# A fused two-layer transformer kernel: token rows spread by DMA, doubled weight buffers, and more of the attention's maxima in the first stage

## The reference

```python
xn = layernorm(x)                                  # no gain, no bias
# first layer, attention branch: 16 heads of width 8, rotary positions
Q, K, V = rope(xn @ Wq.T), rope(xn @ Wk.T), xn @ Wv.T
s = softmax(causal(Q @ K.T / sqrt(8))) @ V @ Wo.T
# first layer, gate branch: feed-forward with weights that depend on the batch
lt   = xn[:, 1:17, :]; even, odd = lt[:, ::2], lt[:, 1::2]          # 8 rows each
m1   = (even[:, :4, :, None] * odd[:, :4, None, :]).reshape(B, 512, 128)
m2   = (even[:, 4:, :, None] * odd[:, 4:, None, :]).reshape(B, 128, 512)
h    = gelu(xn @ W1.T + scale * xn @ m1.T + b1)
g    = silu(h @ W2.T + scale * h @ m2.T + b2)
x    = x + s * g
# second layer: retention with decay, and a mixture of 8 experts (top 2, capacity); x = x + s2 * silu(experts)
```

## Time and profile before

| | |
|---|---|
| Time, 3 runs | 978.13 us median (975.89 to 981.47) |
| Profiled execution, its own time | 978.77 us |
| Its span in the profile | 977.0 us |
| PE busy | 856.4 us (88%) |
| DVE busy | 801.8 us (82%) |
| ACT busy | 725.9 us (74%) |
| POOL busy | 289.4 us (30%) |
| First block | 0 to about 122 us |
| First score product of the second block | 141.93 us |

### The profile page before, as it was taken

How to read it: one execution, slowest core, us unless ns; L and a number is a source line. 1 busy time by engine, 2 the same in 40 slices (tenths; PEclk the granted TensorE clock), 3 DMA queues, 4 the chain that set the end, 5 groups by cost and what they waited for, 6 DMA issues and landing times. The chain is left out here.

```text
span 977.0 us, 25280 instructions
## 1 busy us (share of the span) xinstructions
PE 856.4 (88%) x9413; PEld 459.8 (47%) x9414; DVE 801.8 (82%) x1697; ACT 725.9 (74%) x1493; POOL 289.4 (30%) x329
## 2 busy tenths in 40 slices
PE   3999989899999999999998899888999999889960
PEld 3666533333333333333334777533444444368850
DVE  6665899899999999999963664599999999837895
ACT  2655338788888888888886555688999999958841
POOL 3866311111111000000013676501444442005560
PEclk9999959999999999999999899889999999989985
DMA  5469691744444363333006778596654442546727
GB/s 172 184 261 342 261 219 49 212 103 104 107 104 106 70 137 69 71 67 73 13 14 179 247 236 246 143 224 131 111 118 89 100 82 49 139 147 219 206 104 260
DMA packets 119385, 140.92 MB, mean 144 GB/s; under 512 B 20109, under 2 KB 82138, under 8 KB 118624
## 3 DMA queue, kind: packets, MB, share of 16 engines
q1 hardware_dynamic: 113888, 127.45, 48.3%
q0 software_dynamic: 5376, 11.85, 4.2%
HBM read 77.63 MB, written 63.25 MB: 144 GB/s over the span
## 5 line engine op out<-in xcount | busy, mean ns | idle before, releaser
L980 ACT ACTIVATE probsB<-psB 128x512 f32<-128x512 f32 (+2 forms) x640 | 309.5, 569 | 69.9 <-PE psB L1037 45.1
L174 DVE TENSOR_REDUCE mxB<-psB 128x1 f32<-128x512 f32 x428 | 246.1, 645 | 11.5 <-PE psB L151 8.1
L1030 PE MATMUL psB<-q_groups,k_groups 64*128 64x512 bf16 (+3 forms) x768 | 203.6, 331 | 17.6 <-DVE mxB L174 8.3
L151 PE MATMUL psB<-k_groups,q_groups 64*128 64x512 bf16 (+2 forms) x740 | 206.4, 339 | 2.0 <-PEq L408 1.8
L1058 PE MATMUL psB<-probsB,vB 128*32 128x512 f32 (+3 forms) x1536 | 164.9, 501 | 1.3 <-ACT outB L967 0.6
L1870 ACT ACTIVATE psD<-psD 128x896 f32<-128x896 f32 (+2 forms) x192 | 153.5, 799 | 8.5 <-PE psD L1924 8.3
L1030 PEld LDWEIGHTS psB<-q_groups,k_groups 64*128 64x128 bf16 x768 | 66.8, 94 | 160.9 <-ACT probsB L980 140.2
L1799 DVE TENSOR_REDUCE sumsD<-psD 128x1 f32<-128x128 f32 (+3 forms) x256 | 113.4, 484 | 7.2 <-PE psD L1947 5.0
L1924 PE MATMUL psD<-k_groups,q_groups 64*128 64x512 bf16 (+3 forms) x384 | 103.2, 341 | 13.5 <-ACT psD L1870 5.4
L174 DVE TENSOR_REDUCE mx2B<-psB 128x2 f32<-128x256 f32 (+3 forms) x188 | 102.7, 597 | 11.7 <-PE psB L158 9.6
L158 PE MATMUL psB<-hideB,chooseB 64*128 64x128 bf16 x984 | 108.5, 207 | 0.0
(11 more groups left out here) (239 smaller groups left out, 1551.2 us busy)
## 6 DMA issues: line engine op xcount, KB each, us to landing
v<-vaugA SPq DMA_DIRECT2D x4, 2048.0 KB, 8.8
vB<-v SPq DMA_DIRECT2D x16, 512.0 KB
q_groups<-q SPq DMA_DIRECT2D x32, 200.0 KB
k_groups<-k SPq DMA_DIRECT2D x32, 200.0 KB
back<-emptyB POOLq DMA_DIRECT2D x16, 256.0 KB, 3.8
q<-hiA SPq DMA_DIRECT2D x12, 256.0 KB, 6.6
k<-hiA SPq DMA_DIRECT2D x12, 256.0 KB, 5.9
q_groups<-q SPq DMA_DIRECT2D x32, 96.0 KB
```

The source lines that it names most:

```text
L151: ins = nc.tensor.matmul(bank[:, to:to + w], self.q[r, s, a, t * P:t * P + P], self.k[r, s, a, HALF * c:HALF * c + w], start=True, stop=(c ...
L174: return nc.vector.tensor_reduce(dst, src, AX.X, ALU.max)
L980: nc.scalar.activation(probs[:, n % DEEP, 0:w], st[ring_of(n)][:, 0:w], ACT.Exp, scale=DH ** -0.5).then_inc(exp_done, 1)
L1030: ins = nc.tensor.matmul(bank[:, to:to + w], k[half[r], s, hq // 2, jt * P:jt * P + P], q[half[r], s, hq // 2, i0:i0 + w], start=True, sto ...
```

## The change

- `outer`, its constant and its load are gone. ACT issues two transfers for each batch: one stores the 8 rows from `xn` to DRAM (after the second tile of `normalise`), one reads them back to all partitions of a new tile `first` (`spread_first`). `weights` takes `first` in place of the PSUM banks; both of its tensor operands are then in SBUF.
- `w1e` and `w2e` have two buffers. On DVE `weights(b)` comes right after `rope(b, 0)`, ahead of `statistics(b+1)`; for the first batch it comes ahead of `rope(0, 0)`. PE does `project(0, 1)` inside the first feed-forward.
- `project` waits for one half of `xnT` a product. ACT runs one gelu at the start, and the gelus of the first half batch come ahead of the cast of `hi`.
- 32 units of maxima are in the first block. Units 0 to 7 are in feed_forward(2, 1), in banks 0 and 1 alone; DVE reads them after `weights(3)`. Each pair of them waits until the pair before it has been read. The other 24 stand where 24 stood.
- `vaug` and its DRAM copy have 16 columns a head in place of 32; the weight load of the products with the values still takes 32 columns, and so the next head's 16 as well. A load brings eight pieces of 256 bytes a partition. POOL clears the 16 columns behind the last head.
- DVE's clearing of the tile moves with `EARLY`, to ahead of the 17th unit counted from 32, which is behind the cast L888. In the fourth block the first load of values is issued by ACT.

```diff
+VC = 2 * DH
...
-EARLY = 24
+EARLY, EARLIEST = 32, 8
...
-        w1e, w2e = m.sb("w1eA", [P, FF]), m.sb("w2eA", [P, FC, P])
+        w1e, w2e = m.sb("w1eA", [P, 2, FF]), m.sb("w2eA", [P, 2, FC, P])
...
-        early_banks = [ps[:, i, :] for i in (0, 1, 4, 5)]
+        early_bank = [ps[:, n % 2, :] for n in range(EARLIEST)] + [ps[:, (0, 1, 4, 5)[n % 4], :] for n in range(EARLIEST, EARLY)]
...
                 def weights(b):
                     dve.wait_ge(xnT_ready, 2 * b + 1)
                     V.tensor_scalar(odd[:, :], xnT[:, b % 2, 2:18:2], scale[:, 0:1], None, ALU.mult).then_inc(odd_ready, 1)
-                    dve.wait_ge(outer_done, b + 1)
-                    if b:
-                        dve.wait_ge(u_done, 2 * b)
+                    dve.wait_ge(first_moved, 32 * (b + 1))
+                    if b >= 2:
+                        dve.wait_ge(u_done, 2 * b - 2)
                     dve.wait_ge(odd_ready, b + 1)
                     for j in range(4):
                         c = slice(j * P, j * P + P)
-                        V.scalar_tensor_tensor(w1e[:, c], ps[:, 0, c], odd[:, j:j + 1], w1[:, c], ALU.mult, ALU.add)
+                        V.scalar_tensor_tensor(w1e[:, b % 2, c], first[:, c], odd[:, j:j + 1], w1[:, c], ALU.mult, ALU.add)
                     for j in range(4):
                         o = slice(j * 32, j * 32 + 32)
-                        ins = V.scalar_tensor_tensor(w2e[:, :, o], ps[:, 1, j * P:j * P + P].rearrange("p (r q) -> p q r", q=FC),
+                        ins = V.scalar_tensor_tensor(w2e[:, b % 2, :, o], first[:, HALF + j * P:HALF + j * P + P].rearrange("p (r q) -> p q r", q=FC),
                                                      odd[:, 4 + j:5 + j], w2[:, :, o], ALU.mult, ALU.add)
                     ins.then_inc(w_ready, 1)
...
+                def read_early(first, last):
+                    for n in range(first, last):
+                        dve.wait_ge(groups.max_done, n + 1)
+                        groups.read_maximum(nc, 0, MAX_UNITS[n], early_bank[n]).then_inc(groups.max_read, 1)
...
                 for b in range(B):
                     if b:
                         add_bias(b - 1, 0)
+                    if b == 0:
+                        weights(b)
                     rope(b, 0)
-                    if b == 0:
+                    if b:
                         weights(b)
                     if b + 1 < B:
                         statistics(b + 1)
+                    if b == B - 1:
+                        read_early(0, EARLIEST)
                     if b:
                         add_bias(b - 1, 1)
-                        weights(b)
                     rope(b, 1)
...
-                read_early(0, EARLY // 2)
+                read_early(EARLIEST, EARLIEST + 12)
...
+                        if t == 1:
+                            act.wait_ge(xn_ready, NT * b + 1)
+                            act.dma_start(A["first"][b].rearrange("o (j c) -> (o j) c", c=D), xn[1:17:2, 0, :]).then_inc(first_moved, 16)
+
+                def spread_first(b):
+                    act.wait_ge(first_moved, 32 * b + 16)
+                    if b:
+                        act.wait_ge(w_ready, b)
+                    act.dma_start(first[:, :], A["first"][b].broadcast_to((P, 8 * D))).then_inc(first_moved, 16)
...
+                act.wait_ge(ready, 1)
+                nc.scalar.activation(warm[:, :], eps[:, :], ACT.Gelu)
                 normalise(0)
+                spread_first(0)
                 columns(0)
                 act.wait_ge(ready, 5)
                 act.wait_ge(loaded, 16 * (len(consts) + 2))
                 for b in range(B):
                     keep_v(b)
+                    gelu(b, 0)
                     if b == 0:
                         first_part(0, 0)
-                    gelu(b, 0)
                     if b + 1 < B:
                         normalise(b + 1)
                         columns(b + 1)
                     first_part(b, 1)
                     second_part(b, 0)
+                    if b + 1 < B:
+                        spread_first(b + 1)
                     second_part(b, 1)
...
-                def outer(b):
-                    for j in range(8):
-                        ins = nc.tensor.matmul(ps[:, j // 4, (j % 4) * P:(j % 4) * P + P], pick[:, j, :], xn[:, 0, :],
-                                               start=True, stop=True)
-                    ins.then_inc(outer_done, 1)
-
                 def project(b, half):
                     for j in range(2):
+                        pe.wait_ge(xnT_ready, 2 * b + (1 + j if half == 0 else 2))
                         ins = nc.tensor.matmul(ps[:, 4 + j, :], w_proj[:, j, :], xnT[:, b % 2, halves[half]], start=True, stop=True)
                     ins.then_inc(projected, 1)
...
-                    if n == 2:
+                    if n == EARLIEST + 2:
                         pe.wait_ge(terms_ready, 2 * B)
-                    if n >= 4:
-                        pe.wait_ge(groups.max_read, n - 2)
-                    side_by_side(*(groups.fill_maximum(nc, 0, MAX_UNITS[i], early_banks[i % 4], groups.max_done) for i in (n, n + 1)))
+                    if n:
+                        pe.wait_ge(groups.max_read, n if n <= EARLIEST else n - 2)
+                    side_by_side(*(groups.fill_maximum(nc, 0, MAX_UNITS[i], early_bank[i], groups.max_done) for i in (n, n + 1)))
 
                 def feed_forward(b, half):
                     first = 2 * FC * b + FC * half
                     for c in range(FC):
+                        if b == B - 2 and half == 1 and c % 2:
+                            two_maxima(c - 1)
                         if b == B - 1 and half == 1:
-                            two_maxima(8 + 2 * c)
+                            two_maxima(EARLIEST + 8 + 2 * c)
                         if first + c >= 2:
                             pe.wait_ge(gelu_done, first + c - 1)
-                        nc.tensor.matmul(ps[:, 2 + c % 2, :], w1e[:, c * P:c * P + P], xnT[:, b % 2, halves[half]],
+                        nc.tensor.matmul(ps[:, 2 + c % 2, :], w1e[:, b % 2, c * P:c * P + P], xnT[:, b % 2, halves[half]],
                                          start=True, stop=True).then_inc(h_done, 1)
+                    if b == half == 0:
+                        pe.wait_ge(terms_ready, 1)
+                        project(0, 1)
                     pe.wait_ge(v_kept, 2 * b + half + 1)
                     for t in range(4):
+                        if b == B - 2 and half == 1 and t % 2:
+                            two_maxima(4 + t - 1)
                         if b == B - 1:
-                            two_maxima(16 * half + 2 * t)
+                            two_maxima(EARLIEST + 16 * half + 2 * t)
                         for c in range(FC):
                             if t == 0:
                                 pe.wait_ge(gelu_done, first + c + 1)
                             ins = nc.tensor.matmul(ps[:, 6 + half, t * P:t * P + P], hT[:, c, t * P:t * P + P],
-                                                   w2e[:, c, :], start=(c == 0), stop=(c == FC - 1))
+                                                   w2e[:, b % 2, c, :], start=(c == 0), stop=(c == FC - 1))
                     ins.then_inc(u_done, 1)
                 pe.wait_ge(loaded, 16 * (len(consts) + 2))
                 turn_rows(0)
-                outer(0)
-                pe.wait_ge(xnT_ready, 2)
                 project(0, 0)
                 values(0)
-                pe.wait_ge(terms_ready, 1)
-                project(0, 1)
                 for b in range(B):
                     pe.wait_ge(w_ready, b + 1)
                     feed_forward(b, 0)
                     if b + 1 < B:
                         pe.wait_ge(terms_ready, 2 * b + 2)
                         turn_rows(b + 1)
-                        outer(b + 1)
-                        pe.wait_ge(xnT_ready, 2 * b + 4)
                         project(b + 1, 0)
...
-                    sp.dma_start(v[:, s, :, :], A["v0"][b].rearrange("p (t f) -> p t f", t=NT)[
-                        :, :, s * 4 * VW:(s + 1) * 4 * VW]).then_inc(in_loaded[s], 16)
+                    sp.dma_start(v[:, s, 0:NT * 4 * VC].rearrange("p (t f) -> p t f", t=NT), A["v0"][b].rearrange(
+                        "p (t f) -> p t f", t=NT)[:, :, s * 4 * VC:(s + 1) * 4 * VC]).then_inc(in_loaded[s], 16)
...
+                nc.gpsimd.memset(v[:, :, NT * 4 * VC:], 0.0).then_inc(loaded, 1)
...
-                        ins = nc.tensor.matmul(pv[VW * hq:VW * hq + VW, HALF - w:HALF], v[:, s, jt, VW * hq:VW * hq + VW],
+                        ins = nc.tensor.matmul(pv[VW * hq:VW * hq + VW, HALF - w:HALF], v[:, s, VC * (4 * jt + hq):VC * (4 * jt + hq) + VW],
...
-                load_values(0)
...
+                act.dma_start(v[:, 0, :, 0:D], A["v1"][0].rearrange("p (t c) -> p t c", c=D)).then_inc(v_loaded[0], 16)
```

25 lines of the change are left out of this document (9 added, 16 removed).

## The result

The changed kernel took 994.35 us (median of 4 runs, 990.7 to 995.08) beside 979.8 us of the kernel before: ratio 1.0146, 95% interval 1.0102 to 1.019. A later comparison of the same two gave 1.016 (1.0129 to 1.019). It is 14 to 15 us slower. The profiled execution took 994.29 us, with a span of 992.5 and a mean clock of 0.939 (before 0.948).

The account below looks back on a forecast made before the run. In first-block batches ACT and POOL bound up to the third feed-forward product, then PE without a gap. Terms -1.8 + 6.4 + 8.25 + 3.7 - 4.9 = +11.65 on 978.77 gave 990.4, 990 expected shown; range 974 to 997.

Parts of the forecast that it names:

- Weights from SBUF take turns with POOL: Second and third batch: DVE's weights alternate with POOL until +14.3, so `values` waits 3.2 us each: +6.4 (0 to 12).
- The eight maxima: Third batch's second half: second pair waits for DVE's read behind the weights, delaying the last feed-forward: +8.25 (3.75 to 11).
- Clock: Three new PE idle stretches over 2.6 us lower the granted clock, 1.6 us each: +3.7 (0 to 4.9).
- Start: First batch: PE gets weights 5.3 us earlier, but the third product only 1.8: -1.8 (-5.3 to 0).
- `outer` in steady batches: Removing `outer` gains 0 per steady batch: the third product still waits for the gelu at +6.7.
- Second block's start: Prologue reads 8 units fewer and clearing moves, so the first score product comes earlier: -4.9 (-6.2 to -2.2).
- gives nothing back: Second block after its start: bound by PE and DVE, so it returns none of the shift.
- the fourth rival: Packed values don't shorten the second block's start, 2.2 instead of 4.9: 993; counted within the forecast's range, no separate chance.
- The load of values on ACT's queue "at nothing": Fourth block's first value load, with halved value stores, runs on queues no engine waited for: -0.6 to 0.

Follow-up runs that it names:

- PSUM experiment: Changed kernel without maxima in the third batch, further changed so the weights' first operand in batches 2 to 4 comes from PSUM by `outer`: ratio 0.999 to the kernel before.
- weights last: Changed kernel with the weights of batches 2 to 4 put back behind the bias, SBUF operand and both buffers kept: ratio 1.0019 to the kernel before.
- all together: Changed kernel with weights late, PSUM operand in batches 2 and 3, fourth block's values on SP's queue, second block's rows placed before two loads: 971.35 us, ratio 0.9941.
- placing the rows first: Changed kernel with weights of batches 2 to 4 behind the bias, and second block's rows placed ahead of the second and third value loads: ratio 1.0032 to kernel before.

## Why the prediction was right, and which steps of it were not

**Weights from SBUF take turns with POOL: right in mechanism, +6.4 predicted, 5.0 found.** In the third batch they ended 13.8 us behind the turning's start (predicted 14.3) and `values` started at +16.9 (17.4). The waits were 0.82 and 2.50 in one profile, 2.48 and 2.48 in the other. The 0.82 is short because PE had just lost 1.7 us to the lower clock (3.66 instead of 1.99 at 38.35) and came to `values` that much later: DVE's bias was the bound either way, and 0.82 + 1.7 is the 2.5 of the other profile. So the term is 5.0. The PSUM experiment shows the cause.

By the rule of the Trainium skill ("SBUF — State Buffer", section "Who interferes with whom") a VectorE instruction with two SBUF inputs contends with a GpSimd instruction that reads SBUF. The traces agree for this instruction too, 128 columns at a time: four took 3.92 beside POOL and 1.14 without it.

**The eight maxima: right.** Predicted +8.25 and some clock; the stretch from the turning to the last feed-forward grew by 10.4 (9.8), of which some 2.2 is clock. The 7.05 wait was for DVE's read behind the weights, as said, and moving those weights alone gave 6 to 8 us back. That the maxima cost the first block more than they save in the second is shown by leaving them out (5.4 faster), with the weights in this order. With the weights last the pair waits 0.83, and the kernel with all together is faster than the one before with the maxima in it; no run left them out in that order, so what they bring there isn't known.

**Clock: +3.7 predicted, some 4.0 found beside the waits.** In the third batch the products behind the wait took 0.7 (74.82) and 1.1 us (the eight products behind them, 4.87 instead of 3.79) more than at the upper level, and behind the wait of 7.05 the fourth product took 2.07 instead of 1.12, and the small products 1.92 for eight instead of 1.16 and 2.56 for sixteen instead of 2.05 (half of the 4.11 for 32). The 1.7 at 38.35 stood behind no new wait of `values`: PE had waited 1.94 for a gelu there. It cost nothing of its own, since it only took the place of a wait for DVE.

**Start: -1.8 predicted, -4.0 (-3.3) found.** The weights came 7.1 earlier, not 5.3, since the spread row landed by 16.9 instead of 19.1. That part of the gain is lost on the way to the third product was right: 3.1 of 7.1 went, where 3.5 of 5.3 had been put.

**`outer` in steady batches: 0, right.** The third product stands 6.7 behind the turning's start (64.67 less 57.95) as before; PE waits 1.75 there instead of 0.46.

**Second block's start: -4.9 predicted, -3.8 found.** From the last bias' store (121.40 and 135.14) to the first score product it was 20.5 and is 16.8. The cast was ready at 143.77, and SP went on issuing the three loads until 146.62: 7.50 us for half the bytes, in pieces of 256 instead of 512, where it was 7.37. Of the issue the fourth rival was right; its price, 2.2 instead of 4.9, was too low. That the issue was in the way is shown by placing the rows first: the first score product came 2.9 sooner. By the Trainium skill ("DMA: Bandwidth & Descriptors", section "Specifications") pieces of 256 bytes are under the 512 that line rate needs. The rows show only that halving the bytes did not shorten the issue; the rate itself was not measured.

**That the second block "gives nothing back": right.** The shift falls from +10.0 to +6.7 only against the first profile of before, with its long stretch of 368.0 us. Three profiles of kernels with this second block as before have the first score product at 141.93, 142.40 and 141.58 and start the fourth block at 625.41, 623.47 and 622.30; three with the changed one have them at 151.90, 151.15 and 150.73, and at 632.11, 632.11 and 632.20. The mean shift is 9.3 at the score product and 8.4 at the fourth block, and the step between is one long stretch spread over three.

**The load of values on ACT's queue "at nothing": wrong, and here luck helped the total.** The fourth block took 233.5 us in the profile before and 243.5 after. The 10 us are two things, a late landing and the clock, and only a part of the first is this step's.

The landing: the first product with values waits for this load. Whether it comes early goes by two things over the 14 profiles:

| first product with values, us behind the block's start | load on SP's queue | load on ACT's queue |
|---|---|---|
| no packet of queue q8 in the first 10 us | 5.1, 5.7, 5.4, 6.4 | 7.8, 7.0, 7.7 |
| one of 16 KB, begun 1.8 to 2.7 us behind the start | 8.6 | 9.9, 10.0, 10.4, 11.3, 10.7, 10.4 |

The profile gives this queue the kind `instruction`. The kernel before has such packets 6.7 us ahead of the block's start and 13.3 us behind it, and none between. The changed kernel has one in the first 10 us (packets, MB, share of 16 engines; q10 is the load, and q14 is there in both kernels):

```profile
q10 hardware_dynamic: 1040, 0.52, 23.0%
q14 instruction: 1, 0.01, 0.6%
q8 instruction: 1, 0.02, 0.6%
```

In like kernels ACT's queue costs 1.9 us, and the mean of the kernels with this packet lies 2.9 higher on either queue. The seven with the packet are the seven in which ACT spreads the rows of all four batches, so it may come from ACT's longer program; no run moved the packet alone, and that it causes the delay is not shown. For the queue there are pairs with one edit between them: the kernel before became 3.6 us slower (1.6 to 5.7), the changed kernel with the load back on SP's queue had 1.0150 beside 1.0146 and 1.016, and the kernel with the operand in PSUM gained 1.6.

The second thing is the clock: the granted clock of 10 us stretches behind the start, first of the changed kernel (PE's busy time, clock, DMA share, GB/s),

```profile
632.10:642.10 10.00, 4.64 (x35) 0.52 0.91 192
642.10:652.10 10.00, 9.03 (x93) 0.50 1.00 236
...
672.10:682.10 10.00, 9.75 (x88) 0.59 0.54 90
...
692.10:702.10 10.00, 10.00 (x95) 0.57 0.14 27
```

and of the kernel before:

```profile
625.40:635.40 10.00, 8.63 (x66) 0.52 0.91 195
635.40:645.40 10.00, 8.44 (x103) 0.80 1.01 216
...
665.40:675.40 10.00, 8.13 (x87) 0.83 0.60 95
```

Ten of the 14 profiles fit a length of 228 to 229 us and the landing. The first profile of the changed kernel and two of faster kernels (values on either queue) took 5 more, with low clock up to 70 us behind the start, and a fourth 2 more. The second profile of the changed kernel fits the ten, so this part differs between executions of one kernel; whether the change makes it more frequent, so few profiles can't tell.

I had cleared the edit because no engine waited for that queue; what counts is that the load was the first of 25 in one queue and became one beside 24. The Trainium skill ("DMA: Bandwidth & Descriptors", section "🔬 Queues, rings and completion order") says that a DMA engine goes round between the queues with work; that would make the load late, and no run here shows the packets' order.

**The sum.** Up to the first score product the terms found are -4.0 for the start, 5.0 for the waits, 8.2 for the maxima, 4.0 of clock and -3.8 for the second block, together 9.4 where the profile has 10.0 and the prediction 11.65. The three terms of the mechanism were good; the start and the second block were missed by 2.2 and 1.1 in opposite directions. The measured 14 to 15 were met because a landing 4.5 us later on the mean (9.9 and 10.0 against 5.1 and 5.7), which the prediction hadn't foreseen, made up for it. That is luck. The rest is not pinned down: the one repeated profile is 10 us longer than the two of the kernel before (987.2 against 977.0 and 977.3) while the medians differ by 14 to 15.

## What to carry to other kernels

Moving an operand from PSUM to SBUF to save PE an idle 1.8 us can cost DVE far more: look first at what POOL does beside the instruction. And what is put ahead of a queue's latency-critical item (DVE's bias, DVE's read) is to be priced at its contended length, since PE pays it again in clock. A load that is issued "on an idle queue" still shares the DMA engines: being first in a full queue brought it 1.9 us sooner here. And before a mean over profiles of different kernels is put down to one edit, compare like kernels: over all of them the queue seemed to be worth 3.2.

## What the runs showed of the hardware

- Four DVE instructions of 128 columns beside POOL's instructions: 1.13 us with one operand in PSUM, 3.92 with both in SBUF. POOL's two sums lost only 0.1 (2.60 against 2.50): nearly all of the waiting was DVE's.
- With POOL idle the four of `w1e` take 1.14 us from SBUF, and the four of `w2e`, in another order of columns, 1.47 to 1.50. From one operand in PSUM they take 1.13 and 1.12 also beside POOL.
- An instruction on 8 columns (`odd`, its tensor and its scalar in SBUF) took 0.60 to 1.14 us beside POOL's instructions on 512 columns, in the kernel before too (1.01 in its last batch), and 0.11 to 0.23 elsewhere.
- Three loads of values took SP 7.27, 7.37 and 7.75 us to issue at 512 bytes a piece, and 6.86 to 7.50 at 256 in nine profiles.
- In the fourth block the product that waits for a load of 512 KB came 2.9 us later on the mean in the profiles in which a 16 KB packet of an `instruction` queue fell beside it (not shown to be the cause).
- The fourth block's clock took different courses in two executions of the changed kernel, worth 5 us in one block.
